# Gate shifts as rows for each batch, the first unit's projection in front, and new orders on GpSimd, ScalarE and VectorE, in an adaLN block of two recurrences

## The reference, cut to what matters

```
mod = (silu(c) @ wmod).reshape(8, 6, 1, 256)
sa, ca, ga, sb, cb, gb = mod[:, 0..5]         # ga, gb: magnitude at least 0.25
h = layernorm(x) * (1 + ca) + sa
# first layer, over 1024 steps: h_t = tanh(h_(t-1) @ A.T + x_t @ B.T); y_t = h_t @ C.T
x = x + ga * (layernorm(y + h) * gamma + beta)
h = layernorm(x) * (1 + cb) + sb
# second layer; it scans its first axis, which is the batch of 8, with 1024 rows side by side
f = sigmoid(h_b @ wf.T + c @ uf.T + bf); i = sigmoid(h_b @ wi.T + c @ ui.T + bi)
g = tanh(h_b @ wc.T + c @ uc.T + bc);    c = f * c + i * g
x = x + gb * tanh(h_b @ wo.T + c_final @ uo.T + bo)
```

## Time and profile before

| what | value |
|---|---|
| three executions | 627.73, 630.47, 630.78 us, median 630.47 |
| the profiled execution | 629.32 us, span 627.5 us |
| TensorE matmul busy | 569.3 us, 91% |
| VectorE, ScalarE, GpSimd busy | 428.9, 346.9, 352.9 us (68, 55, 56%) |
| mean granted TensorE clock | 0.958 |
| loop one ends, unit 7 begins | about 157 us |
| DMA, x to xin, issue to landing | 2.8 us |
| DMA, table to tA, issue to landing | 4.5 us |

### The profile page before, as it was taken

One profiled execution on the slowest core, in us unless ns is written; L12 is line 12 of the kernel. 1 busy time (PEld: TensorE's weight loads), 2 busy tenths in 40 slices (PEclk: granted clock), 3 DMA queues, 4 the chain that ended last, 5 costly groups with the idle time before them and its releaser, 6 DMA issues.

```text
span 627.5 us, 14012 instructions
## 1 busy us (share of the span) xinstructions
PE 569.3 (91%) x4674; PEld 556.5 (89%) x4674; DVE 428.9 (68%) x1030; ACT 346.9 (55%) x867; POOL 352.9 (56%) x481
## 2 busy tenths in 40 slices
PE   6399999899998999999999999999999998998940
PEld 4399999889897999999999999999999998888930
DVE  4689999986353766555677677766777757556655
ACT  2367777768234655555555655565555564555431
POOL 3556666665244454454377765667756765764421
PEclk9689999999787999999999999999999999999975
DMA  6736444423223222221224223343223423321433
GB/s 212 182 104 205 144 142 141 141 86 108 78 71 94 66 83 80 76 60 60 70 68 148 89 85 95 107 119 103 86 88 109 138 72 88 115 68 57 84 70 120
DMA packets 58656, 64.44 MB, mean 103 GB/s; under 512 B 5432, under 2 KB 49632, under 8 KB 58592
## 3 DMA queue, kind: packets, MB, share of 16 engines
q1 hardware_dynamic: 58592, 63.63, 34.4%
HBM read 46.80 MB, written 16.81 MB: 101 GB/s over the span
## 4 chain that ended last, share of the span: by engine, by line
PE 49%; issue 19%; POOL 17%; DVE 6%; ACT 4%; DMA 3%; POOLq 0%; SPq 0%; DVEq 0%; ACTq 0%
PE psI L1278 7%; PE psF L1278 6%; PE psG L1278 6%; PE psR L1241 6%; PE psW L1325 3%; PE psR L1165 3%; PE psC L1267 3%; POOL wx L590 3%; POOL wx L614 2%; PE psO L1201 2%; PE psF L1165 2%; PE psW L1360 2%; DVE hin L931 2%; POOL xin L597 2%; POOL rstdB L625 2%
## 5 line engine op out<-in xcount | busy, mean ns | idle before, releaser
L1044 DVE SCALAR_TENSOR_TENSOR lo<-psT,cb1T,hi 128x256 fp32r<-128x256 f32 x64 | 28.0, 480 | 85.6 <-ACT hi L741 85.6
L1241 PE MATMUL psR<-hs,AT 128*128 128x128 f32 x432 | 64.5, 282 | 9.4 <-ACT hs L712 6.4
L622 POOL TENSOR_TENSOR veB<-mvB,epst 128x2 f32<-128x2 f32 x32 | 6.3, 197 | 117.8 <-DVE mvB L991 117.8
L569 POOL TENSOR_TENSOR hin<-hin,uvec 128x256 f32<-128x256 f32 x64 | 47.2, 760 | 36.6 <-ACT hin L697 36.6
L1241 PEld LDWEIGHTS psR<-hs,AT 128*128 128x128 f32 x432 | 56.1, 194 | 11.4 <-ACT hs L712 7.2
L723 ACT ACTIVATE zn<-state,nmA,rstdA 128x256 f32<-128x256 f32 x64 | 35.0, 594 | 50.1 <-POOL nmA L606 50.1
L723 ACT ACTIVATE xn<-state,nmB,rstdB 128x256 f32<-128x256 f32 x64 | 35.0, 595 | 35.1 <-POOL nmB L628 35.1
L580 POOL TENSOR_TENSOR hsl<-hs,hsh 128x512 fp32r<-128x512 f32 x32 | 41.9, 1308 | 22.0 <-ACT hsh L719 22.0
L617 POOL TENSOR_TENSOR zn<-zn,tA 128x512 f32<-128x512 f32 x32 | 41.4, 1293 | 13.3 <-ACT zn L723 13.3
L1165 PE MATMUL psR<-hs,AT 128*128 128x128 f32 x192 | 40.4, 293 | 7.3 <-DVE wx L861 7.0
L931 DVE SCALAR_TENSOR_TENSOR hin<-xin,mvA,uvec 128x256 f32<-128x256 f32 x64 | 41.5, 687 | 2.3 <-DMA h_park<-hin 0.7
(11 more groups left out here) (251 smaller groups left out, 2403.6 us busy)
## 6 DMA issues: line engine op xcount, KB each, us to landing
xin<-in_L_attn_x_dram SPq DMA_DIRECT2D x32, 256.0 KB, 2.8
h_park<-hin SPq DMA_DIRECT2D x32, 256.0 KB, 2.2
hin<-h_park SPq DMA_DIRECT2D x64, 128.0 KB
xin<-in_L_attn_x_dram SPq DMA_DIRECT2D x64, 128.0 KB
tA<-rows_d SPq DMA_DIRECT2D x32, 256.0 KB, 4.5
out_dram<-state SPq DMA_DIRECT2D x64, 128.0 KB
tW<-rows_d SPq DMA_DIRECT2D x32, 128.0 KB, 4.2
tG<-rows_d SPq DMA_DIRECT2D x24, 128.0 KB, 4.3
```

Source lines behind the costliest of these rows:

```text
L569: pool.tensor_tensor(h, h, sa, ALU.add).then_inc(a_h, 1)
L1044: dve.scalar_tensor_tensor(lo[:, (n + 1) % 2, k, :], psT[:, k * POS:(k + 1) * POS], cb1T[:, k, (n + 1) % NB:(n + 1) % NB + 1], hi[:, (n + ...
L1241: ins = pe.matmul(ps, AT[:, k, m * P:(m + 1) * P], hs[:, k, :, (t - 1) % 4, :], start=(k == 0 and (separate or m == 0)), stop=(k == H - 1 ...
```

## The change

What it does:

- **TensorE.** The shift of gate i is now `shift_row(i)`: the table of 8 columns is the stationary operand and the weights of 256 columns move, 12 fp32r matmuls a gate, result with the batches on 8 partitions (gates f and i in psW, gate c in psI). ScalarE copies the rows to shr, and `shift_columns` turns them with six transposes of 8 x 128 into the columns of biasT. The tables get a split for it (sbT_hi, sbT_lo, c0z_hi, c0z_lo). Row 0 stands in unit 7, rows 1 and 2 in unit 8. Tile c4 of the projection moves from unit 9 to unit 8, and in unit 8 the first project (c2) stands ahead of step 16. The wait for biasT moves from times_wo(0) to gate_x(0, 1).
- **VectorE.** `split_tables` moves from behind step 15 to behind step 14 in unit 7. In unit 8, tile c2 and mvA(0) come ahead of step 16, and x1(0), its statistics and tile c4 come in unit 8. mvA(m) comes ahead of the projected tiles (but for m = 8, 16, 24). x1(m) and its statistics come ahead of wx and gf, with fin between the two, and gf comes ahead of wx.
- **GpSimd.** low(u) waits for fin(o) (or for x1(m) while there is no o). ua is done one tile ahead, behind low, and waits for the fin before. xg of the next tile comes at the end of the unit.
- **ScalarE.** tanh(2u) comes ahead of xn(m-1).
- **SP.** load_h(4) is issued with the first loads.

The diff, cut to its core:

```diff
-    CSEQ = [(0, 0, 0, 7), (0, 0, 2, 7), (0, 1, 0, 8), (0, 0, 4, 8), (0, 0, 6, 9), (0, 1, 2, 9), (0, 1, 4, 10), (0, 1, 6, 11)]
+    CSEQ = [(0, 0, 0, 7), (0, 0, 2, 7), (0, 1, 0, 8), (0, 0, 4, 8), (0, 0, 6, 8), (0, 1, 2, 9), (0, 1, 4, 10), (0, 1, 6, 11)]
...
# SP
                     load_h(3)
+                    load_h(4)
                 for c, (_, _, _, at) in enumerate(CSEQ):
-                    if c >= 4 and at == u + 2:
+                    if c >= 5 and at == u + 2:
...
# GpSimd, unit2
-                if has(o, 0, LAST):
-                    pool.wait_ge(s_wx, o + 1)
-                    pool.wait_ge(s_u, o // NB + 1)
-                    t = wx[:, o % NWX, :]
-                    pool.tensor_tensor(t, t, uvec[:, :], ALU.add).then_inc(s_ua, 1)
+                if u == ML:
+                    xg_of(0)
                 if u == ML + 1:
                     low(ML)
-                if norm:
...
+                    xg_of(1)
...
                 if has(u, U0, PAIRS - U0) and u != ML:
+                    if o >= 0:
+                        pool.wait_ge(s_fin, o + 1)
+                    elif norm:
+                        pool.wait_ge(s_x1, m + 1)
                     low(u)
+                if has(o + 1, 0, LAST):
+                    if o >= 0:
+                        pool.wait_ge(s_fin, o + 1)
+                    pool.wait_ge(s_wx, o + 2)
+                    pool.wait_ge(s_u, (o + 1) // NB + 1)
+                    t = wx[:, (o + 1) % NWX, :]
+                    pool.tensor_tensor(t, t, uvec[:, :], ALU.add).then_inc(s_ua, 1)
...
+                if has(m, 1, NU - 2):
+                    xg_of(m + 1)
# ScalarE, unit2
-                if has(m - 1, 1, NU - 1):
-                    xn_of(m - 1)
+                if u == ML + 1:
+                    ng_of(0)
+                    xn_of(0)
                 if rec:
                     step(2 * u)
                 if u == ML + 1:
-                    ng_of(0)
                     high(ML)
-                    xn_of(0)
+                if has(m - 1, 1, NU - 1):
+                    xn_of(m - 1)
...
+                if u == ML:
+                    for i, src in enumerate((psW[0:NB, :], psI[0:NB, 0:D])):
...
# VectorE, split_tables
+                dve.tensor_copy(sbT_hi[:, :, :], sbT[:, :, :]).then_inc(q_sbc, 1)
...
+                dve.tensor_copy(c0z_hi[:, :, :], c0z[:, :, :]).then_inc(q_sbc, 1)
...
# VectorE, unit2
+                if u == ML:
+                    projected_tiles(here[0])
+                    mean_var(0)
                 if rec:
                     step(2 * u)
-                if u == ML + 1:
-                    scaled_rows(0)
+                if u == ML - 1:
+                    split_tables()
...
+                if has(m, 1, NU - 1) and m % NB:
+                    mean_var(m)
+                if u == ML:
+                    projected_tiles(here[1])
+                elif here:
                     projected_tiles(here[0])
...
+                if u == ML:
+                    scaled_rows(0)
+                    row_stats(0)
+                    projected_tiles(here[2])
...
+                if u == XL - 1:
+                    dve.wait_ge(q_shc, 1)
+                    dve.tensor_tensor(biasT[:, :, :, :], psI[:, D:D + 3 * H * NB].rearrange("p (n m b) -> p n m b", n=3, m=H),
...
+                if has(m, 1, NU - 1):
+                    scaled_rows(m)
                 if has(o, 0, NU):
...
+                if has(m, 1, NU - 1):
+                    row_stats(m)
                 if has(n, 0, NU):
-                    dve.wait_ge(s_W, n + 1)
-                    dve.wait_ge(s_tW[n % 2], 16 * (n // 2 + 1))
-                    dve.tensor_tensor(two(wx[:, n % NWX, :]), two(psW[:, :]), both(tW[:, n % 2, :]), ALU.add).then_inc(s_wx, 1)
                     dve.wait_ge(s_f, 2 * n + 2)
...
+                    dve.wait_ge(s_W, n + 1)
+                    dve.wait_ge(s_tW[n % 2], 16 * (n // 2 + 1))
+                    dve.tensor_tensor(two(wx[:, n % NWX, :]), two(psW[:, :]), both(tW[:, n % 2, :]), ALU.add).then_inc(s_wx, 1)
-                if has(m, 1, NU - 1):
-                    scaled_rows(m)
# TensorE
+                if n == 0 and i == 1:
+                    pe.wait_ge(q_bias0, 1)
...
-                pe.wait_ge(q_sbc, 3)
+                pe.wait_ge(q_sbc, 7)
...
-            def shift(i):
-
-                for m in range(H):
-                    at = D + (i * H + m) * NB
-                    n = 0
-                    for name, few in ((("wf", "wi", "wc")[i], sbT), (("uf", "ui", "uc")[i], c0z)):
-                        for k in range(H):
-                            for w in (whi, wlo):
-                                n += 1
-                                last = pe.matmul(psW[:, at:at + NB], w[name][:, k, m * P:(m + 1) * P].bitcast(f32), few[:, k, :],
-                                                 start=(n == 1), stop=(n == 8))
+            def shift_row(i):
+
+                ps = (psW[0:NB, 0:D], psW[0:NB, D:W], psI[0:NB, 0:D])[i]
+                n = 0
+                for name, shi, slo in ((("wf", "wi", "wc")[i], sbT_hi, sbT_lo), (("uf", "ui", "uc")[i], c0z_hi, c0z_lo)):
+                    for k in range(H):
+                        for w, few in ((whi, shi), (whi, slo), (wlo, shi)):
+                            n += 1
+                            last = pe.matmul(ps, few[:, k, :], w[name][:, k, :], start=(n == 1), stop=(n == 12))
                 last.then_inc(q_gb, 1)
+
+            def shift_columns():
+                pe.wait_ge(q_shr, 2)
+                for i in range(3):
+                    for m in range(H):
+                        at = D + (i * H + m) * NB
+                        last = pe.transpose(psI[:, at:at + NB], shr[:, i, m * P:(m + 1) * P], ident[0:NB, 0:NB])
+                last.then_inc(q_shc, 1)
...
+                if u == ML:
+                    project(here[0])
                 if rec:
                     step(2 * u)
-                if here:
+                if u == ML:
+                    project(here[1])
+                    shift_row(1)
+                elif here:
                     project(here[0])
...
-                if u == XL - 3:
+                if u == ML - 1:
                     project(here[1])
                     shift_wo()
-                    shift(0)
-                if u == XL - 2:
-                    project(here[1])
-                    shift(1)
+                    shift_row(0)
+                if u == ML:
+                    shift_row(2)
+                    project(here[2])
                 if u == XL - 1:
-                    shift(2)
                     tokens(0)
+                    shift_columns()
```

More of the change, by code:

```diff
@@ L581, in low, with xg_of @@
                                    ALU.subtract).then_inc(s_hsl, 1)
+            def xg_of(m):
+                pool.wait_ge(s_x[m % 2], 32 * (m // 2 + 1))
+                pool.wait_ge(s_tA[m % 2], 16 * (m // 2 + 1))
+                xg = two(xin[:, m % 2, :])
+                pool.tensor_tensor(xg, xg, both(tA[:, m % 2, D:W]), ALU.add).then_inc(s_xg, 1)
             def unit2(u):
@@ L977, in projected_tiles, with mean_var, row_stats @@
                     dve.bn_stats(stA[:, T % 2, 2 * (b + i) + j, :], halfw(z, i)).then_inc(s_stA, 1)
-            def scaled_rows(m):
-                dve.wait_ge(s_zg, m + 1)
-                dve.tensor_tensor(tiles_of(m), two(zn[:, :]), two(xin[:, m % 2, :]), ALU.add).then_inc(s_x1, 1)
+            def mean_var(m):
+                dve.wait_ge(s_stA, 2 * max(projected(m // NB, j, m % NB // 2 * 2) for j in range(2)))
+                dve.wait_ge(s_nA, m)
+                apart(dve)
+                for j in range(2):
+                    dve.bn_aggr(mvA[:, j, :], stA[:, m // NB % 2, 2 * (m % NB) + j, :]).then_inc(s_mvA, 1)
+            def row_stats(m):
                 dve.wait_ge(s_x1, m + 1)
@@ L991, in scaled_rows @@
                     dve.bn_aggr(mvB[:, j, :], stB[:, j, :]).then_inc(s_mvB, 1)
+            def scaled_rows(m):
+                dve.wait_ge(s_zg, m + 1)
+                dve.tensor_tensor(tiles_of(m), two(zn[:, :]), two(xin[:, m % 2, :]), ALU.add).then_inc(s_x1, 1)
             def unit2(u):
@@ L1012, in unit2 @@
                     dve.tensor_tensor(cst[:, :, :], i2, gf[:, :, :], ALU.add).then_inc(s_c, 1)
-                if here:
-                    projected_tiles(here[0])
-                if has(m, 0, NU):
-                    dve.wait_ge(s_stA, 2 * max(projected(m // NB, j, m % NB // 2 * 2) for j in range(2)))
-                    dve.wait_ge(s_nA, m)
-                    apart(dve)
-                    for j in range(2):
-                        dve.bn_aggr(mvA[:, j, :], stA[:, m // NB % 2, 2 * (m % NB) + j, :]).then_inc(s_mvA, 1)
+                if has(m, 1, NU - 1) and m % NB:
[3 more added lines that the diff above has]
+                elif here:
+                    projected_tiles(here[0])
+                if has(m, 1, NU - 1) and m % NB == 0:
+                    mean_var(m)
```

38 lines of the change are left out of this document (18 added, 20 removed).

## The result

Four executions of the changed kernel took 602.89 to 605.38 us, median 603.52. The kernel before took 627.73 to 630.78 in four, median 629.95. The ratio is 0.959 with a 95% interval of 0.956 to 0.962: 26.4 us faster, where 22.3 were forecast.

A forecast was written before the change was run, and what follows sets the result against it. TensorE was taken to bound units 11 to 31, so gains lie in the start, units 19 and 27, and late units: 12.0 + 2.3 + 8.0 = 22.3 us off the 630.5 median, giving 608.2 us, range 602 to 619.

The forecast's parts named there:

- Part 1, the start: Units 7 to 11: shift rows, earlier projected tile and new orders gain 12.0 us, ends 7 and 14.5.
- The walk: Start traced through all engines at full clock: step 23 starts at 197.7 instead of 210.76, gain 13.0 us.
- "-1.0" for 0.6 of a fall of the clock: Start: allowance of 1.0 us lost to half clock behind TensorE's idle 2.3 us, at about 1.7 per fall.
- the rival at 13 in 100: Start: the clock falls as before, three falls return and cost 5 us, giving 613 us; 13 in 100.
- The sum by the rule: Whole kernel: if activity releases the clock throttle, the start runs at full clock and the sum is 1.0 us better.
- Part 2, units 19 and 27: Tanh ahead of xn and an earlier mvB remove TensorE's waits for tanh: 2.3 of 2.6 us, ends 0 and 2.6.
- Part 3, the late units: Units 35 to 40: GpSimd's ring falls under TensorE's unit, 11.95 to 10.6 us each; gain 8.0, ends 1 and 9.5.
- Part 4, costed at nothing: Units 11 to 31: GpSimd's new waits for fin are covered, thinnest 1.6 us at hsl; cost nothing.
- a ring of the late units that stays: Late units: gate F waits 1.1 again or hi is pushed, leaving 1 of 8 us: 615 us; 12 in 100.
- GpSimd's ring didn't outgrow TensorE's unit: Rival, units 19 to 31: GpSimd's ring, 11.8 us, exceeds TensorE's 13.34 if adds run slow; no change or slower; 9 in 100.
- That every wait goes: Rival: start gains 14.5, late units 9.5, units 19 and 27 2.6; 26.6 us off, 604 us; 10 in 100.
- the ring's 9.5: Late units: the chain through GpSimd and VectorE shortens from 11.95 to 9.5 us a unit.

The follow-up runs named there:

- Experiments 10 and 12: Changed kernel with x1(1), its statistics and ngB(1) moved behind step 20: 602.83 us; the same plus 22 unread matmuls before the last final state's product: 602.77 us.
- Experiments 3 and 4: Changed kernel with 16 unread fp32 products of 8 moving columns added in unit 22: 610.89 us; with 30 unread matmuls of the new row form instead: 606.62 us.
- Experiment 8: Changed kernel with ScalarE's xn(m-1) ahead of tanh(2u) again: 607.74 us.
- experiments 5, 6 and 7: Changed kernel with GpSimd's ua back between nmB and xg: 607.58 us; with x1 and statistics last on VectorE again: 607.75 us; with both back: 614.97 us.
- the kernel with the rows alone: Kernel before the change with only the shift rows, in the old shifts' places in units 7, 8 and 9: 620.39 us.
- experiment 9: Changed kernel without GpSimd's waits for fin and x1 ahead of low and ua, orders kept: 611.34 us.

## Why the prediction was right, and where it was off

**The bound.** Right. Units 11 to 31 were TensorE's and stayed so, 262.07 of 262.07 us busy.

**Part 1, the start.** Right in mechanism, and 1.0 short in size. The walk gave 13.0 at full clock and 13.0 came; its times held to within about half a microsecond, once loop one's 0.6 is taken off. The step that failed is the "-1.0" for 0.6 of a fall of the clock. A whole fall did come, behind an idle 2.6 us that was forecast at 2.3, and made step 21 and gate I take 1.8 us more (1.69 for 0.9, 2.45 for 1.42). But the walk has TensorE ready at 193.0 and gate F(1) waiting for gf until 194.9, and this wait of 1.9 swallowed it: 0.7 of it is left. The loss was counted on top of a path that ran through VectorE. Experiments 10 and 12 agree: both starts take 42.4 us, with a wait for gf of 1.7 where the clock didn't fall and of 0.7 where it did.

Two readings behind this part are wrong, without harm to its sum. A gate's old shift is 16 products, not 32: the x32 of the earlier trace rows are passes, so there were 48 products and 96 passes in all. And the first of the old falls came in the middle of shift(0), not behind it: its pairs of passes follow each other every 0.22 us up to 165.0 and every 0.43 from 165.3 on, and so it took 5.17 us for 3.47. This fall lasted 6.8 us, the two others 3.4.

That the clock's falls would go with the narrow products was treated as open (the rival at 13 in 100). Experiments 3 and 4 settle that it was the form of the products (few columns in fp32), not the busy share.

**The rule weighed there.** The Trainium skill ("TensorE: Matmul & The Clock Gate", What's actually happening) has it that activity releases the throttle. Experiment 3 goes against the simple reading of it: 6.90 of 6.90 us busy with 0.51 granted. The tail goes with it in part: idle, then 0.55; filled, then 1.00; but idle, then 1.00 in two other profiles. The decision to go by the measured falls was right. The sum by the rule would have been 1.0 better and by accident nearer.

**Part 2, units 19 and 27.** Right size (2.5 for 2.3); the cause is only bounded. The prediction gave it to the place of xn and, in passing, to the earlier mvB. Experiment 8 puts xn back and loses 0.4 of it; experiments 5, 6 and 7, which keep xn's new place and undo other orders, keep all but 0.1 of it; only the kernel with the rows alone has the old 12.21. So the place of xn suffices without the ring's two orders, and isn't needed where they stand, the rest of the change being there both times. Which of the other moves does it without xn's wasn't tried one by one.

**Part 3, the late units.** The mechanism was right, shown by experiment 7. The step that failed is a term of the sum: "TensorE's own unit is the old one less its waits for gf and cst: 11.95 - 1.1 - 0.3 = 10.5", and the late 10.6 built on it. It measured 10.14. The waits of the earlier trace rows are counted from the modelled ends of the matmuls, which overlap. From start to start the same two gaps were 1.24 to 1.43 and 0.42 to 0.51 us before, where matmuls now follow each other every 0.11, and the first matmul behind each held up the next by another 0.08 and 0.03. That is 1.8 us a unit for the 1.4 taken off. And the allowance for hi and for a late gf wasn't needed: TensorE is busy 60.06 of 60.30 us. Five times 0.46 is 2.3, which with the first late unit (1.4 for 1.2) is the whole 2.4 that was missed.

**Part 4, costed at nothing.** The cost was right, the account of the benefit was not. The waits cost nothing in units 11 to 31, which keep their 13.3 us. But "0.9 us of VectorE that nobody waits for" was wrong: under the new orders x1, fin and gf stand on the path in the start, in unit 27 and in the late units, and there the waits are worth 7.8 us (experiment 9). I had counted the gain of parts 1 and 3 with x1 and fin at 0.7 and so used the effect of the waits without crediting them with it.

**The rivals.** The clock falling as before and a ring of the late units that stays are excluded by the stage view and by the 10.14. GpSimd's ring didn't outgrow TensorE's unit: (281.52 - 214.70) / 5 = 13.36 us for times_wo to times_wo:

```profile
214.70 1.41 PE psW L1372 x12
...
281.52 1.42 PE psW L1372 x12
```

That every wait goes came nearest in time, with a different make-up: gaps of 0.8, 1.3, 2.8 and 1.0 us from matmul to matmul stayed in the start, and the late units came within 0.6 of the ring's 9.5.

## What to carry to other kernels

When a stage's bound is to pass from one ring to another engine, work out the new bound from the starts of that engine's instructions, not from the old period less its listed waits, for these leave out the handovers. Don't add a loss of one engine to a walk in which that engine waits for another behind it. Give an operation of VectorE with two SBUF operands a moment in which GpSimd is still, by order or by a wait, wherever somebody waits for it: here the wait cost nothing and the overlap nearly a microsecond each time. And turn an fp32 product with a handful of moving columns round, so that the few columns are the stationary operand of an fp32r product.

## What the runs showed of the hardware

- 16 fp32 products with 8 moving columns, in a stretch where TensorE was wholly busy before, during and behind, brought 6.9 us at a granted clock of 0.51, beginning while they still ran. 30 matmuls with 8 stationary and 256 moving columns at the same place left it at 1.00. That busy time isn't enough to keep the clock I hadn't expected.
- Such a row matmul costs no more than one with 128 stationary columns: 30 made unit 22 longer by 3.4 us, and from start to start they follow each other every 0.12, as the twelve of project do in 1.42. Its weight load is 88 ns.
- A VectorE add of 128x512 fp32 with both operands in SBUF took 0.68 us alone and 1.60 to 1.76 in four pairs with a GpSimd operation of the same size. GpSimd's own operation took its usual 1.26 to 1.29 in three of them and 1.73 in the fourth, and 1.78 to 1.80 in nine meetings with VectorE's clo.
- 2.7 us with TensorE nearly idle were followed by 3.5 us at 0.55, and in the same place filled with matmuls the clock stayed at 1.00 and the tail was 1.5 us shorter. The fall doesn't always come: two of twelve profiles with the idle stretch stayed at 1.00.
